# Three products of rounded parts in a projection, and a feed-forward that shares its rounding and adding out among the engines

## The reference, cut to what matters

```python
def bitlinear(x, W, b):
    w_scale = jnp.clip(jnp.mean(jnp.abs(W)), EPS, None)
    Wq = jnp.clip(jnp.round(W / w_scale), -1.0, 1.0) * w_scale
    x_scale = jnp.clip(jnp.max(jnp.abs(x), axis=-1, keepdims=True), EPS, None)
    xq = jnp.clip(jnp.round(x * (QB / x_scale)), -QB - 1.0, QB) * (x_scale / QB)
    return jnp.einsum('bnd,hd->bnh', xq, Wq) + b
...
x = x + bitlinear(gelu(bitlinear(layernorm(x), W1, b1)), W2, b2)     # 256 -> 1024 -> 256
...
latents = layernorm(layernorm(x)) * ln_l_g + ln_l_b
q, k, v = latents @ Wq.T, *split(latents @ Wlkv.T)                    # 256 -> 3 * 256
```

## Time and profile before

| what | value |
|---|---|
| median of 3 runs | 929.03 us (927.93 to 929.19) |
| the profiled execution | 928.22 us, its span 926.5 us |
| PE busy | 866.8 us, 94% |
| DVE busy | 630.7 us, 68% |
| ACT busy | 532.6 us, 57% |
| POOL busy | 388.9 us, 42% |
| chain that ended last, PE's share | 67% |
| the same, DVE's, ACT's and POOL's | 17%, 6%, 2% |

### The profile page before, as it was taken

One profiled execution on the slowest core, in us unless ns is written; L12 is line 12 of the kernel. 1 busy time (PEld: TensorE's weight loads), 2 busy tenths in 40 slices (PEclk: granted clock), 3 DMA queues, 4 the chain that ended last, 5 costly groups with the idle time before them and its releaser, 6 DMA issues.

```text
span 926.5 us, 14997 instructions
## 1 busy us (share of the span) xinstructions
PE 866.8 (94%) x4299; PEld 611.3 (66%) x4300; DVE 630.7 (68%) x1275; ACT 532.6 (57%) x851; POOL 388.9 (42%) x334
## 2 busy tenths in 40 slices
PE   9977789889999999999999999999999999999992
PEld 4635455545555555555457887878888888888881
DVE  5788987855567557456488779846666666666666
ACT  2558885445665765775554534326666666666650
POOL 2144455435676746756515545512222222222210
PEclk9999999989999999999999999999999999999997
DMA  9400000009478578569565100078711298526405
GB/s 310 110 1 1 0 1 1 1 5 364 160 292 328 194 305 326 219 269 350 199 262 196 82 1 1 12 316 342 305 40 36 71 348 341 208 88 254 116 9 182
DMA packets 49909, 154.07 MB, mean 166 GB/s; under 512 B 6266, under 2 KB 24438, under 8 KB 44236
## 3 DMA queue, kind: packets, MB, share of 16 engines
q1 hardware_dynamic: 46124, 144.25, 41.4%
q0 software_dynamic: 3744, 9.31, 3.1%
HBM read 97.85 MB, written 56.62 MB: 167 GB/s over the span
## 4 chain that ended last, share of the span: by engine, by line
PE 67%; DVE 17%; ACT 6%; issue 3%; DMA 3%; POOL 2%; SPq 1%; DVEq 0%; ACTq 0%; POOLq 0%
PE banks L1047 11%; PE banks L1300 8%; PE banks L1302 8%; PE banks L1301 8%; PE banks L1015 4%; PE banks L1039 3%; PE banks L1040 3%; DVE small L2105 2%; PE banks L1337 2%; PE banks L1339 2%; PE banks L1338 2%; PE banks L1313 2%; PE banks L953 2%; PE banks L919 1%; PE banks L1061 1%
## 5 line engine op out<-in xcount | busy, mean ns | idle before, releaser
L1047 PE MATMUL banks<-wexp 128*65 128x512 f32 (+1 forms) x288 | 149.9, 602 | 3.5 <-ACT wexp L1614 3.5
L677 POOL TENSOR_TENSOR cv_hl<-wexp,cv_hl 128x1024 fp32r<-128x1024 f32 x45 | 108.6, 2421 | 56.0 <-ACT cv_hl L1591 55.4
L1300 PE MATMUL banks<-ring,x_hi 128*128 x312 | 127.5, 408 | 0.0
L1302 PE MATMUL banks<-ring,x_lo 128*128 x312 | 122.1, 391 | 0.0
L1301 PE MATMUL banks<-ring,x_hi 128*128 x312 | 122.0, 391 | 0.0
L1614 ACT ACTIVATE wexp<-banks 128x512 f32<-128x512 f32 x128 | 76.4, 599 | 64.2 <-PE banks L1040 63.8
L2105 DVE TENSOR_REDUCE small<-banks 128x1 bf16<-128x1107 f32 x64 | 84.1, 1314 | 38.4 <-PE banks L1015 38.4
L1750 ACT ACTIVATE banks<-wexp 128x1024 f32 x72 | 73.5, 1021 | 47.7 <-DVE aux L2496 47.7
L1728 ACT ACTIVATE aux<-banks 128x512 f32<-128x512 f32 x78 | 46.7, 599 | 61.2 <-PE banks L1302 45.2
L1039 PE MATMUL banks<-q_hi,k_hl 128*128 128x512 f32 x144 | 76.7, 533 | 1.9 <-ACT q_lo L1582 1.0
L1302 PEld LDWEIGHTS banks<-ring,x_lo 128*128 128x128 f32 x312 | 58.6, 188 | 13.2
(11 more groups left out here) (374 smaller groups left out, 2171.5 us busy)
## 6 DMA issues: line engine op xcount, KB each, us to landing
wsplit<-cv_hl SPq DMA_DIRECT2D x45, 1024.0 KB, 8.0
ring<-wsplit SPq DMA_DIRECT2D x32, 1280.0 KB
wexp<-in_L_ffn_w SPq DMA_DIRECT2D x40, 512.0 KB, 5.9
wexp<-in_expert_biases SPq DMA_DIRECT2D x8, 1152.0 KB, 6.6
ring<-wsplit SPq DMA_DIRECT2D x4, 1024.0 KB, 8.2
wexp<-moe_y SPq DMA_DIRECT2D x7, 512.0 KB, 6.1
wexp<-in_L_ffn_sw SPq DMA_DIRECT2D x5, 512.0 KB, 9.0
x_sb<-in_x SPq DMA_DIRECT2D x4, 512.0 KB, 7.6
```

Source lines behind the costliest of these rows:

```text
L677: g.tensor_tensor(sides(hl[:, PIECE:2 * PIECE]), raw, sides(hl[:, 0:PIECE]).bitcast(f32), ALU.subtract).then_inc(s['cv_lo'], 1)
L1047: mm(pb[5 + half][0:DA, :], vh[b][0:w, c, :], pT[q % 3][0:w, :], start=c == 0, stop=c == len(KTILES) - 1).then_inc(s['a_pv'], 1)
L1300: mm(o[:], x_hi[u][:, kc, :], hi, start=kc == 0 and not primed, stop=False, skip_group_check=primed)
L1302: last = mm(o[:], x_lo[u][:, kc, :], hi, start=False, stop=primed and kc == KC - 1, skip_group_check=primed)
```

## The change

In the feed-forward:
- POOL rounds the tokens of tile t-1 after it has normalized tile t (ACT still does it for the last tile), normalizes by multiply and add (with a new small array `less_mean`, one more DVE instruction in each of two places) instead of subtract and multiply, and adds the result of tile t-6 into `x_sb`. The last six of these additions stand behind the scale for tiles 0 to 7 and before all of POOL's projection work.
- ACT copies the second product out of PSUM with its scale into one of two `y_part` buffers (`ffn_sum`), at the head of its turn. DVE's `ffn_sum` is gone, and its statistics of a tile come one turn later, at the end of the turn.
- PE turns the tokens between the second product and the hidden values, and no more at the head of the turn.
- The constants of the attention are written within POOL's tiles 8 to 12.

In the projection:
- the float32 product becomes three products of float32r parts: high tokens by high weights, high by low, low by high. ACT makes the high weights in one copy in turn -4, POOL the low weights (256 x 768 values) in its tiles 7 and 9.
- Tokens are turned in pairs of tiles. ACT scales a pair out of PSUM twice, into `l_hi` (rounded) and `xnT`, and DVE subtracts (`proj_low`) to get `l_lo`; the low products of a tile's first part wait for it.
- `proj_low` stands on DVE behind turn 12's `proj_tokens`, behind turn 14, and then behind the squares of tiles 2, 4, ..., 12.
- The scale for tiles 8 to 15 takes its root from ACT and six short DVE instructions behind tile 2, instead of fourteen behind tile 3.

```diff
--- before.py
+++ after.py
+        _, l_hi, l_lo, w_hi, w_lo = aliased(("x_span16", XS), *((n, KC * 4 * P) for n in ("l_hi", "l_lo")), *((n, KC * QKV) for n in ("w_hi", "w_lo")))
+        l_hi, l_lo, w_hi, w_lo = (v[:].rearrange("p (a b) -> p a b", a=KC) for v in (l_hi, l_lo, w_hi, w_lo))
...
+        W_LOW_AT = (7, 9)
...
+            def ffn_tokens(t):
+                g.tensor_scalar(xn[:, t % 2, :], xn[:, t % 2, :], f_by[:, t % 2, 0:1], MAGIC, ALU.mult, ALU.add).then_inc(s['f_xm'], 1)
+
+            def ffn_result(t):
+                pool.wait_ge(s['f_yout'], t + 1)
+                g.tensor_tensor(x_sb[:, t, :], x_sb[:, t, :], y_part[t % 2], ALU.add).then_inc(s['f_res'], 1)
+
+            def attention_constants(k):
+                if k == 4:
+                    link(g.memset(o_hi[DH:P, :].bitcast(f32), 0.0))
+                elif k % 2:
+                    link(g.memset(k_hi[k // 2][DH:DA, 0:S + SK].bitcast(f32), 1.0))
+                else:
+                    link(g.memset(k_hl[k // 2][:, S + SK:KW].bitcast(f32), 0.0))
+                    link(g.memset(vh[k // 2][:, :, DH:DA], 1.0))
+
             for t in range(T):
                 if t == TB:
                     pool.wait_ge(s['f_rstd'], 2)
                 if t >= 2:
                     pool.wait_ge(s['f_xqT_full'], t - 1)
-                g.tensor_scalar(xn[:, t % 2, :], x_sb[:, t, :], mv[:, t, 0:1], rstd[:, t:t + 1], ALU.subtract, ALU.mult).then_inc(s['f_xn'], 1)
+                g.tensor_scalar(xn[:, t % 2, :], x_sb[:, t, :], rstd[:, t:t + 1], less_mean[:, t:t + 1], ALU.mult, ALU.add).then_inc(s['f_xn'], 1)
+                if t >= 1:
+                    pool.wait_ge(s['f_by'], t)
+                    ffn_tokens(t - 1)
+                if t in W_LOW_AT:
+                    pool.wait_ge(s['w_pre'], 3)
+                    kc = W_LOW_AT.index(t)
+                    g.tensor_tensor(w_lo[:, kc, :], wT[:, kc, :], w_hi[:, kc, :].bitcast(f32), ALU.subtract).then_inc(s['w_pre'], 1)
                 pool.wait_ge(s['f_xn'], t + 1)
-                if t >= 5:
-                    pool.wait_ge(s['f_by'], t)
                 g.tensor_tensor(x_sb[:, t, :], x_sb[:, t, :], b2_all[:], ALU.add).then_inc(s['f_pool'], 1)
+                if t >= 6:
+                    ffn_result(t - 6)
+                if 8 <= t < 13:
+                    pool.wait_ge(s['f_res'], t - 5)
+                    attention_constants(t - 8)
 
             x, y, d = (r[:, 0:LN_EARLY] for r in (root_a, root_s, root_t))
             link(g.tensor_copy(d, x.bitcast(i32)))
@@ -629,13 +665,10 @@
                 link(g.tensor_scalar(d, d, -0.5, 1.5, ALU.mult, ALU.add))
                 link(g.tensor_tensor(ln_r[:, 0:LN_EARLY] if k == 2 else y, y, d, ALU.mult))
             pool.sem_inc(s['f_pool'], 1)
-
-
-            for u in range(2):
-                link(g.memset(k_hl[u][:, S + SK:KW].bitcast(f32), 0.0))
-                link(g.memset(k_hi[u][DH:DA, 0:S + SK].bitcast(f32), 1.0))
-                link(g.memset(vh[u][:, :, DH:DA], 1.0))
-            link(g.memset(o_hi[DH:P, :].bitcast(f32), 0.0))
+            for t in range(T - 6, T):
+                ffn_result(t)
...
+            def ffn_tokens_T(t, u):
                 pe.wait_ge(s['f_xm'], t + 1)
                 for kc in range(KC):
                     last = tr(pb[7][:, kc * P:(kc + 1) * P], xn[:, u, kc * P:(kc + 1) * P], ident[:])
                 last.then_inc(s['f_xqT_full'], 1)
+
+            def ffn_in(t, u):
...
                 if there(i):
                     ffn_out(i, u)
+                if there(i + 4):
+                    ffn_tokens_T(i + 4, u)
                 if there(i + 1):
                     ffn_hidden_T(i + 1, 1 - u)
...
-            def proj_in(t):
-                pe.wait_ge(s['l_xh'], t + 1)
-                if t > 0:
-                    pe.wait_ge(s['l_xT'], t)
+            def proj_in(p):
+                pe.wait_ge(s['l_xh'], 2 * p + 2)
+                if p > 0:
+                    pe.wait_ge(s['l_xT'], 2 * p)
                 for kc in range(KC):
-                    last = tr(pb[7][:, kc * P:(kc + 1) * P], xn[:, t % 4, kc * P:(kc + 1) * P], ident[:])
+                    for u in range(2):
+                        at = (kc * 2 + u) * P
+                        last = tr(pb[7][:, at:at + P], xn[:, (2 * p + u) % 4, kc * P:(kc + 1) * P], ident[:])
                 last.then_inc(s['l_xT_full'], 1)
 
             def proj_part(t, k):
+                p = t // 2
                 if k == 0:
-                    pe.wait_ge(s['l_xT'], t + 1)
+                    if t == 0:
+                        pe.wait_ge(s['w_pre'], 2 + 1 + KC)
+                    pe.wait_ge(s['l_xT'], 2 * p + 1)
                     if t >= 2:
                         pe.wait_ge(s['l_qk'], t - 1)
                 a, n = ((0, 2 * D), (2 * D, D))[k]
+                o, at = pb[PROJ_BANK[t % 2] + k][:, 0:n], slice(t % 4 * P, (t % 4 + 1) * P)
                 for kc in range(KC):
-                    last = mm(pb[PROJ_BANK[t % 2] + k][:, 0:n], xnT[:, kc, t % 4 * P:(t % 4 + 1) * P], wT[:, kc, a:a + n], start=kc == 0, stop=kc == KC - 1)
+                    mm(o, l_hi[:, kc, at], w_hi[:, kc, a:a + n], start=kc == 0, stop=False)
+                    mm(o, l_hi[:, kc, at], w_lo[:, kc, a:a + n], start=False, stop=False)
+                if k == 0:
+                    pe.wait_ge(s['l_xlo'], p + 1)
+                for kc in range(KC):
+                    last = mm(o, l_lo[:, kc, at], w_hi[:, kc, a:a + n], start=False, stop=kc == KC - 1)
                 if k:
                     last.then_inc(s['l_qkv'], 1)
 
             def proj(t):
                 proj_part(t, 0)
                 proj_part(t, 1)
-                if t + 2 < T:
-                    proj_in(t + 2)
+                if t % 2 == 0 and t + 2 < T:
+                    proj_in(t // 2 + 1)
 
             def between(i):
                 if i == -3:
-                    warm(WARM_FFN)
+                    warm(WARM_FFN, pb[5])
                 if i == T - 4:
                     proj_in(0)
...
+            def ffn_sum(t, u):
+                act.wait_ge(s['f_y'], t + 1)
+                act.wait_ge(s['f_by'], t + 5)
+                if not isinstance(t, int) or t >= 2:
+                    act.wait_ge(s['f_res'], t - 1)
+                a(y_part[u], pb[6][:, 0:D], ACT.Copy, scale=f_step[:, 1 - u, 1:2]).then_inc(s['f_yout'], 1)
+
             def ffn_turn(i, u):
-                if there(i + 3):
-                    ffn_T(i + 3, 1 - u)
+                if there(i - 1):
+                    ffn_sum(i - 1, 1 - u)
                 if there(i):
                     ffn_hidden_T(i, u)
                 if there(i + 4) or there(i + 1):
                     ffn_quantise(i + 4, i + 1, i, u)
                 if there(i + 2):
                     ffn_act(i + 2, u)
-
-            def proj_T(t):
-                act.wait_ge(s['l_xT_full'], t + 1)
-                if t >= 4:
-                    act.wait_ge(s['l_qkv'], t - 3)
-                for kc in range(KC):
-                    last = a(xnT[:, kc, t % 4 * P:(t % 4 + 1) * P], pb[7][:, kc * P:(kc + 1) * P], ACT.Identity,
-                             scale=lg[:, kc:kc + 1], bias=lb[:, kc:kc + 1])
-                last.then_inc(s['l_xT'], 1)
+                if there(i + 4):
+                    ffn_T(i + 4, u)
...
+            def proj_T(p):
+                act.wait_ge(s['l_xT_full'], p + 1)
+                if p >= 2:
+                    act.wait_ge(s['l_qkv'], 2 * p - 2)
+                for to in (l_hi, xnT):
+                    for kc in range(KC):
+                        last = a(to[:, kc, pair_at(p)], pb[7][:, kc * 2 * P:(kc + 1) * 2 * P], ACT.Identity,
+                                 scale=lg[:, kc:kc + 1], bias=lb[:, kc:kc + 1])
+                    last.then_inc(s['l_xT'], 1)
 
             def proj_kept(t):
                 act.wait_ge(s['l_qkv'], t + 1)
                 o = PROJ_BANK[t % 2] * 512
                 a(qkv[:, t, :], banks[:, o:o + QKV], ACT.Copy).then_inc(s['l_qk'], 1)
-                if t + 2 < T:
-                    proj_T(t + 2)
+                if t % 2 == 0 and t + 2 < T:
+                    proj_T(t // 2 + 1)
...
+                    a(flat(w_hi), flat(wT), ACT.Copy).then_inc(s['w_pre'], 1)
...
-            def ffn_sum(t, u):
-                ve.wait_ge(s['f_y'], t + 1)
-                ve.wait_ge(s['f_pool'], t + 1)
-                v.scalar_tensor_tensor(tile(t), pb[6][:, 0:D], f_step[:, 1 - u, 1:2], tile(t), ALU.mult, ALU.add)\
-                    .then_inc(s['f_yout'], 1)
-
             def ffn_statistics(t):
-                ve.wait_ge(s['f_yout'], t + 1)
-                statistics(t)
+                ve.wait_ge(s['f_res'], t + 1)
+                return statistics(t)
...
+                if there(i - 2):
+                    last = ffn_statistics(i - 2)
...
+            def proj_low(p):
+                ve.wait_ge(s['l_xT'], 2 * p + 2)
+                if p >= 2:
```

(21 more changed lines are left out.)

79 lines of the change are left out of this document (46 added, 33 removed).

## The result

| | before | after |
|---|---|---|
| median of the runs, us | 929.01 (927.93 to 929.19) | 939.35 (938.01 to 940.57) |
| ratio of after to before | | 1.0113 (95% interval 1.0094 to 1.0133) |
| span of the profiled execution, us | 926.5 | 938.8 |
| mean granted clock of PE | 0.987 | 0.976 |

The page of the changed kernel: its span, busy time by engine, and the clock in 40 slices.

A forecast was written before the change was run, and what follows sets the result against it. Bounds taken: a DVE and ACT ring in the feed-forward, PE briefly in the projection, then DVE. Terms -2.9 - 0.8 + 0.8 + 8.3 + 0.5 = +5.9 on 928.22 gave 934.1, median 934.9 us; range 923 to 941.

The forecast's parts named there:

- The turns: Feed-forward: thirteen turns of the DVE and ACT ring at 4.1 us for 4.32, -2.9 us.
- The first two turns: Feed-forward start, filling the pipeline: each loses ACT's 0.42 us rounding of tokens, -0.8 us.
- POOL's burst: Low weights in POOL's tiles 7 and 9 outrun its slack and make tokens late: +0.8 us (0 to 5).
- POOL's prices: POOL's work in the feed-forward: multiply-and-add 0.7 us, low weights 2.2 us each.
- POOL slow: Rival: POOL's multiply-and-add takes 1.22 us, low weights and constants lie bare, +5.5, 940 us; chance 0.12.
- Factors of turn 13: End of feed-forward: queued on DVE behind pair 0's low part, which waits for ACT; two microseconds late.
- Hand-over: Feed-forward to projection: PE stands 6 us at tile 4 for DVE's low part behind POOL's squares; root of means +5.9.
- From the root to the first maxima: Pair 6 waits for tokens 13, and ACT's four scalings precede the first head's copies: +2.4 us.
- The rival of the clock: Rival: a standing PE falls to its lower clock; one more such stretch costs 1.8, 937 us; chance 0.11.
- The rule weighed: Two-input DVE and POOL instructions exclude each other: 0.5 us per low part, up to 4 more; charged only where named.
- Low parts in time: Rival: pair 2's low part is done when tile 4's high products are issued; -4.1, 925 us; chance 0.20.
- Overlap: Rival: DVE's idle time before the first maxima closes, most of the +8.3 goes; 930 us; chance 0.15.

The follow-up runs named there:

- pairs_tokens: Changed kernel with one float32 product, rows still in pairs, and tokens 9 and 13 made earlier in DVE's queue: 927.31 us.
- singly_reordered: Changed kernel with one float32 product, rows turned singly, no weight parts, hand-over reordered and PE's products of ones ahead of tokens 1: 921.61 us.
- reordered2: Changed kernel, all its work kept, hand-over reordered, tokens and low parts moved in DVE's queue, low weights in tiles 5 and 7: 927.54 us.
- clock_filled: Changed kernel plus 44 unused PE products of ones, behind tile 4's high products and ahead of pair 6's turn: 936.22 us.
- low_early: Changed kernel with DVE's low parts of pairs 2 and 3 taken earlier in its queue: 940.44 us.
- head_and_weights: Changed kernel with PE's 12 products of ones ahead of the turn of tokens 1 and POOL's low weights all in tile 3: 938.84 us.
- tokens13: Changed kernel with DVE making tile 13's tokens along with tile 12's, ahead of the root of the means: 935.89 us.
- squares_first: Changed kernel with POOL adding and squaring tiles 0 and 1 ahead of adding the last feed-forward result: 937.85 us.

## Why the prediction was right in sign, and 4.4 us short

**The turns: right in size, too much in sum.** 4.1 forecast, 4.105 measured, from tile 8 on. But from tile 0 to 14 the gain is 1.6 (62.42 before, 60.85 after), for 2.9 in the sum. Three terms were mis-sized. The first two turns lose 0.9 (10.52 us from tile 0 to tile 2, for 9.66) where -0.8 was forecast: PE's 12 products of ones now stand behind the turn of tokens 1, which waits for POOL, and in this execution they run at the lower clock. The last line is the windows view of pairs_tokens.

```profile
63.32 0.69 PE L936 MATMUL banks<-ident,aux 128*128 128x128 f32 x2 [3.28 <-POOL aux L622]
63.80 5.16 PE L822 MATMUL banks<-ones_b 128*128 128x512 bf16 x12
68.80 1.03 PE L945 MATMUL banks<-wexp,aux 128*128 128x512 bf16 x4
...
62.00:68.00 6.00, 4.74 (x23) 2.33 (x24) 5.59 (x19) 3.30 (x6) 3.40 (x6) 1.00 0.00 1
```

The difference is the clock's: pairs_tokens has the same order there and full clock, and takes 8.90 from tile 0 to tile 2, 0.76 less than before, as forecast. I had not costed the clock at the head.

The twelve turns from tile 2 to tile 14 took 4.40 each before (52.76 in all), not the 4.32 that I read behind tile 8. Without the weights' parts they take 48.80 (singly_reordered), a gain of 4.0 where the sum has 2.9; in the changed kernel they take 50.33. So POOL's burst, +0.8 (0 to 5), costs 1.5. The turn with the second low weights takes 5.0 for 4.0 with none or with them elsewhere (singly_reordered, reordered2), the first some 0.45. Most of the 1.0 is not POOL's time but a wait of DVE in the ring itself, which the low weights had pushed beside a memset:

```profile
94.32 1.01 POOL L632 MEMSET k_hi<- 1x1101 f32 x1
94.40 0.96 DVE L2035 TENSOR_SCALAR small<-small 128x2 f32<-128x2 f32 x1
```

The like step one turn earlier (90.16) takes 0.17. My 4.1 for 4.0 a turn stood for such meetings with POOL's additions; a memset was not in it.

**POOL's prices: right.** Multiply-and-add 0.56 and 0.47 for 0.7, low weights 1.83 for 2.2. The rival "POOL slow" falls.

**Factors of turn 13: too little.** 2 forecast; the step from tile 14 to 15 takes 2.4 more than before (130.33 there) and 3.3 more than without the low part.

**Hand-over: the mechanism seen, its lever not.** The forecast named a stand of 6 us behind tile 4, released by DVE's low part: 6.83. Squares of tile 2 leave POOL at 151.4, which is 152.1 on the forecast's clock, for 151.7, and its order holds on to the root: 9.0 measured for 5.9. Three things fill most of the gap: the half-clock stretch that the stand brings (1.4 by clock_filled), the low part held by POOL (0.9, below), and turn 13 (0.4 more). But the step of the reasoning that failed is the one from "PE stands here" to "this costs": taking the stand away (low_early) gained nothing. The schedule had tokens 9 at 160.3 and "PE turns pair 4 only after them" in it, and I read it as a consequence, when it was the condition; with tokens 9 and 13 put forward, 7.1 us go (in the kernel with one product).

**From the root to the first maxima: 3.6 for 2.4.** The wait for tokens 13 was named; its stretch at the lower clock, from 174 on, was not. The rival of the clock was right as a mechanism (it gave 1.8 a stretch, some 1.5 was measured) and counted once where it comes twice here; 3.1 on top of 934.9 is 938. With the 1.6 at the head (10.52 for 8.90) the clock costs 4.7 us in the profiled execution, where the sum has nothing. The spans, 12.3 apart, exceed the forecast of 5.9 by 6.4; the other misses partly cancel (the turns gained more, POOL's burst and the waits cost more). So what the sum lacked most is PE's clock, a rival to which I had given 0.11.

**The rule weighed.** I priced low parts at 0.69 and let DVE wait for POOL only where named. The group by form of the changed kernel, from 120 to 190 us, against the earlier trace rows:

```profile
L2088 DVE TENSOR_TENSOR l_lo<-aux,l_hi 128x512 fp32r<-128x512 f32 x7 | 5.7, 820 | 5.6 <-ACT aux L1596 5.6
```

One of the seven, at 152.04, takes 1.59 beside POOL's square of 1.05 that starts with it; the others 0.69. So the low parts waited 0.9 in all, not the up to 4 that I worked out from the rule alone; with the 0.8 of the ring's step at 94.40, 1.7 of such waits were found where the sum has nothing for either. The Trainium skill, "SBUF — State Buffer", section "Who interferes with whom", has a VectorE instruction with two SBUF inputs contend with a GpSimd instruction that reads SBUF, and one with at most one input (outside the two-port modes) not at all. head_and_weights agrees: 1.50 and 1.72 for the two-input steps, 0.20 for the reciprocal beside the same POOL work. The steps with one input at 94.40 here, and at 67.91 there (0.65, ending with an addition of POOL), waited too; whether they were in a two-port mode the traces don't show. My fault was to average the waits; they strike where a short step meets a long POOL instruction.

**The other rivals.** Low parts in time (925): POOL's first square came at 147.01, behind the last result, as the forecast had it. Overlap (930): no, the waits did not close, and the way from tile 14 to the first maxima grew by 12.6 where the forecast had 8.3.

## What to carry over

A stand of the busiest engine is not a price: before it is charged, ask what the released engine would meet next, and take out all waits of the chain on paper at once; here three single repairs gave 0, 1.6 and 1.0 us, one moved instruction (tokens 13) 3.8, and two in the kernel with one product 7.1. Ask too at what clock the engine goes on behind a stand, since two such stretches cost 3.1 here. When work is grouped (rows turned in pairs), the group starts with its last member: look where that member's maker stands in its queue before counting what the group saves. And work off the critical path on POOL is not free when a short step of a DVE chain meets it.

## What the hardware showed that was not expected

PE's clock behind a stand has a price of its own: 44 products of ones in the stands made the kernel 3.1 us faster by its first maxima (0.57 to 1.00 in both windows). The stand's length alone doesn't tell whether the clock falls: behind the 3.28 us ahead of 63.32 it is 0.50, behind the same stand in pairs_tokens (3.29) it is 1.00, and behind the 3.34 of tokens13 it is 1.00 too.

The same code of the head ran differently from one profile to the next. Its 12 products of ones took 5.16 us (after), 4.36 (squares_first), 4.06 (low_early) or 2.75 (pairs_tokens), and tile 14 was read at 124.35, 123.63, 122.35 and 122.21. The lower level met those products for nearly their whole length, for a part, or not at all. What sets it was not found. The changed kernel's runs lie near 938 and near 940.5; whether that is the same thing stays open, as the clock by stretch is known for one of them only.
